# Two graph layers of an attention block, worked on two pairs of heads at a time, with all engine queues in a new order

## The chip, the cores and the metric

The kernel runs on one core of a Trainium2 chip. The metric is the device time of one execution in microseconds (us); less is better. TensorE (PE) multiplies, VectorE (DVE) and ScalarE (ACT) work on what it leaves in its accumulators (PSUM, eight banks of 128 partitions x 512 f32), GpSimd (POOL) does elementwise work in SBUF and issues indirect DMAs, SyncE (SP) issues the other DMAs. Every engine has one queue and works it off in order; semaphores tie the queues together.

## The reference

`x` is 16 batches of 256 tokens x 128. An attention block with a small graph network on its value vectors is added to it, then a mixture of experts (8 experts, the best 2 for each token). Cut to what matters here:

```python
xn = layer_norm(_layernorm(x), gamma_in)
q, k, v = (xn @ Wq) * scale, xn @ Wk, xn @ Wv          # 16 heads of 64
attn = softmax(causal(q @ k.T))
out = attn @ v
adj = clip(attn + eye(n), 0, 1)
deg = adj.sum(-1, keepdims=True)
feats = v
for l in range(2):                                     # the two graph layers
    h = feats @ gnn_w[l] + gnn_b[l]
    h = (adj @ h) / deg
    feats = gelu(h + feats)
out = out + feats @ lin_w + lin_b
x = x + layer_norm(out @ Wo, gamma_out)
x = x + moe(rmsnorm(_layernorm(x)))                    # router, top 2 of 8, silu(gate) * up, down
```

## The kernel before

One program without a scheduler: each engine has a function `batch(b, before, routed, after)` that lists, by hand, what this engine does for one batch, and the order of the lines is the order of its queue. Batches 0 and 1 and the last (15) are written out, batches 2 to 14 are one hardware loop. Beside the attention of batch `b` each turn carries the end of the batch before it (its last output products, the norm and residual steps `norm_tokens(before, 0..11)`), the routing of the one before that (`logits`, `choose`, `places`, `place_tokens`, `scatter`) and the input norm of the next one (`norm_step(after, 0..5)`, `x_transposed`, the first `queries_keys` and `values`). After batch 15 comes `sorted_stage`, the experts, in 71 steps of 128 tokens each.

The 16 heads of a batch are eight pairs n = 0 to 7. For a pair: `queries_keys(n)` (six f32r products of 256 columns into bank 0, copied by ACT), `scores(n)` (PE, 12 instructions, into two of the banks 1, 2, 6), `maxima(n, a)` (DVE), `exps(n, a)` (ACT, accumulating the sums), `adjacency(n)` and `weights(n)` (DVE), `graph(n)` and `degrees(n)` (POOL scales the exponentials and spreads the degrees), `transposes(n)` (PE, banks 3 and 4) and their copy `graph(n)` (ACT), `differences(n)` (PE, the graph applied to the values, bank 5) with `degrees(n)` (PE), `difference(n)` and `attended(n)` (DVE), and `mixed_values(n)` (ACT copies the mixed values from bank 5 to `gvT`).

Then the two layers. Before the change they too go pair by pair: `layer1(n)` (PE: `gvT` by the first weights, 256 columns in bank 0), `layer1_out(n)` (DVE adds the values to it, `z1`), `gelu1(n)` (ACT, `f1T`), `layer2_in(n)` (PE, two tiles of 128 columns in bank 2; ACT copies them to `g1`), `layer2(n)` (PE: the graph again, through `mixed`, 256 columns in bank 1), `layer2_out(n)` (DVE, `z2`), `gelu2(n)` (ACT, `f2T`), and `output_graph(n)` (PE, adds into bank 7 beside `output_attended(n)`). An f32 product of 256 columns is recorded as two MATMUL rows. `scores`, `differences` and `layer2` use 64 of the array's rows or columns per instruction, the rest uses 128.

What waits for what, as far as the prediction uses it: `scores(n)` needs `exps(n-1, 0)`, because three banks hold the scores; `differences(n)` needs the copies `graph(n)` and `mixed_values(n-1)`; `layer2(n)` needs ACT's copy of `layer2_in(n)` and `layer2_out(n-1)` of DVE; `output_natural` needs `output_bias` of DVE; POOL's queue waits for `place_tokens(routed, 1)` of DVE ahead of its four `scatter` DMAs. In batch 15 DVE also builds the table of expert steps (`table_first(0..4)`) and the high parts of the expert weights (`gate_up_high(0..7)`), POOL their low parts (`gate_up_low`), each of whose buffers SP refills by DMA when POOL has used it; SP loads the first tokens of the sorted stage (`zin`) when `table_first(4)` is done.

## Time and profile before

| | us |
|---|---|
| median of 3 runs | 1151.72 (1150.24 to 1152.72) |
| the profiled execution, its own time | 1155.31 |
| its span, first to last instruction | 1153.4 |
| PE, DVE, ACT, POOL busy of the span | 1071.1, 884.1, 803.4, 500.3 |
| mean granted clock of TensorE | 0.977 |

The span is what the trace shows; 1.9 us lie around it. Busy shares are averages over three stages: a start of some 20 us, sixteen batches of about 57 us (the last one longer), and the experts from about 958 us on. A row of the timeline has the start in the span, the duration, and in brackets the time that the engine sat idle before it and what ended that. Rows of PE overlap, since the ends are modelled; two starts subtracted tell more than a duration.

### The profile page before, as it was taken

Reading aid. Unit: us, or ns where it says so; the run is one execution under the profiler, and the core shown is the slowest. Engines: PE = TensorE matmul, PEld = TensorE weight load, DVE = VectorE, ACT = ScalarE, POOL = GpSimd, SP = SyncE. Lnnn points to the kernel's source line nnn. Section 1 sums busy time; section 2 is a strip of 40 time slices with the busy share of each in tenths; the row PEclk is TensorE's granted clock in tenths of the full one; section 3 lists DMA queues with packets and bytes.
Section 4 is the critical chain, followed back from the end, with each engine's and each line's share of the span. In section 5 each row is a group of like instructions: output and inputs, shape, how many; then the busy total and the mean of one; then the engine's idle time right before and its main releaser. Section 6 shows DMA issues by size and latency. Waiting matters only on the chain.

```text
span 1153.4 us, 28732 instructions
## 1 busy us (share of the span) xinstructions
PE 1071.1 (93%) x8576; PEld 854.7 (74%) x8576; DVE 884.1 (77%) x3760; ACT 803.4 (70%) x2351; POOL 500.3 (43%) x649
## 2 busy tenths in 40 slices
PE   4899999999999999999999999999999968898993
PEld 3777777777777777777777777777777747898993
DVE  3667797979797979797979797979797984565556
ACT  3668686868686868686868686868787735464551
POOL 3334244434343535353534353535353552544444
PEclk9899999999999999999999999999999988998997
DMA  6970000000000000000000000000000021222227
GB/s 192 405 260 2 1 2 11 1 10 1 10 1 11 1 10 0 10 0 10 0 10 0 10 0 10 0 10 0 10 0 10 2 78 44 56 57 61 59 61 226
DMA packets 37312, 47.43 MB, mean 41 GB/s; under 512 B 6009, under 2 KB 28539, under 8 KB 37200
## 3 DMA queue, kind: packets, MB, share of 16 engines
q1 hardware_dynamic: 32880, 37.81, 10.3%
q0 software_dynamic: 4320, 8.47, 2.2%
q14 instruction: 84, 0.69, 0.2%
q8 instruction: 28, 0.46, 0.2%
HBM read 18.14 MB, written 28.58 MB: 41 GB/s over the span
## 4 chain that ended last, share of the span: by engine, by line
PE 83%; DVE 6%; issue 3%; ACT 2%; SPq 2%; DMA 1%; another core or an unknown queue 1%; POOL 0%; DVEq 0%; POOLq 0%; ACTq 0%
PE bank L635 68%; PE bank L735 3%; PE bank L748 3%; PE bank L774 2%; PE bank L751 2%; PE bank L749 2%; PE bank L1006 2%; DMA x_all<-in_x 1%; PE bank L988 1%; DVE eb L1421 1%; DVE x_all L1995 1%; DVE got L1993 1%; DVE nmax L1406 0%; PE bank L783 0%
## 5 line engine op out<-in xcount | busy, mean ns | idle before, releaser
L497 POOL TENSOR_TENSOR ea<-ea,wgt 128x256 f32<-128x256 f32 x128 | 80.0, 625 | 429.6 <-DVE wgt L1430 396.1
L1406 DVE TENSOR_REDUCE nmax<-bank 128x1 f32<-128x128 f32 (+1 forms) x512 | 152.2, 347 | 66.0 <-PE bank L635 57.1
L499 POOL TENSOR_TENSOR eb<-eb,wgt 128x512 f32<-128x512 f32 x128 | 133.6, 1044 | 0.0
L635 PE MATMUL bank<-gt,g 128*64 128x256 f32 (+1 forms) x1024 | 112.0, 339 | 19.5 <-DVE z L1461 12.0
L1421 DVE SCALAR_TENSOR_TENSOR eb<-idw,ssum,eb 128x256 f32<-128x256 f32 x256 | 129.8, 544 | 0.0
L1124 ACT ACTIVATE ea<-bank,nmax 128x128 f32<-128x128 f32 x256 | 95.8, 374 | 47.9 <-DVE nmax L1406 45.9
L1124 ACT ACTIVATE eb<-bank,nmax 128x256 f32<-128x256 f32 x256 | 123.4, 482 | 0.0
L1092 ACT ACTIVATE gt<-bank 128x512 f32<-128x512 f32 (+1 forms) x256 | 111.7, 493 | 13.3 <-PE bank L751 11.8
L635 PE MATMUL bank<-gt,vnat 128*64 128x256 f32 (+1 forms) x1024 | 110.0, 335 | 3.0 <-issue 0.8
L635 PE MATMUL bank<-qk 64*128 64x128 f32 (+1 forms) x1024 | 112.7, 339 | 0.0
L525 POOL DMA_INDIRECT pairs<-zout,zin x71 | 69.7, 981 | 99.0 <-DVE zout L1954 89.3
L635 PEld LDWEIGHTS bank<-gt,g 128*64 128x64 f32 x1024 | 66.5, 137 | 61.4 <-issue 35.4
L1092 ACT ACTIVATE g<-bank 128x256 f32<-128x256 f32 x128 | 48.8, 381 | 84.8 <-PE bank L635 84.8
L635 PEld LDWEIGHTS bank<-gt,vnat 128*64 128x64 f32 x1024 | 65.1, 136 | 50.2 <-issue 17.0
L1461 DVE TENSOR_TENSOR z<-bank,f1T 128x256 f32<-128x256 f32 x128 | 53.6, 419 | 48.5 <-PE bank L635 48.5
L635 PE MATMUL bank<-xt_lo,w_hi 128*128 128x256 f32 x256 | 87.0, 340 | 1.9 <-DVE xt_lo L1399 1.9
L635 PE MATMUL bank<-gw,f1T 128*128 128x128 f32 x512 | 88.1, 295 | 0.3 <-ACT f1T L1148 0.3
L1947 DVE TENSOR_TENSOR shid<-bank,ssg 128x352 f32<-128x352 f32 x71 | 37.3, 525 | 63.5 <-ACT ssg L1272 40.6
L1092 ACT ACTIVATE qk<-bank 128x512 f32<-128x512 f32 x128 | 78.1, 610 | 11.2 <-PE bank L635 8.9
L635 PEld LDWEIGHTS bank<-gw,f1T 128*128 128x128 f32 x512 | 70.3, 192 | 19.3 <-issue 11.0
L1418 DVE SCALAR_TENSOR_TENSOR ea<-ident,ssum,ea 128x128 f32<-128x128 f32 x256 | 83.2, 362 | 0.0
L1092 ACT ACTIVATE gvT<-bank 128x256 f32<-128x256 f32 x128 | 49.1, 383 | 44.2 <-DVE aT L1440 40.6
(234 smaller groups left out, 3153.0 us busy)
## 6 DMA issues: line engine op xcount, KB each, us to landing
slots<-zero SPq DMA_DIRECT2D x33, 520.0 KB, 15.0
zin<-slots SPq DMA_DIRECT2D x71, 65.0 KB
got<-pairs SPq DMA_DIRECT2D x8, 512.0 KB, 5.5
raw_gu<-in_guT SPq DMA_DIRECT2D x8, 352.0 KB, 3.0
out<-x_all SPq DMA_DIRECT2D x8, 256.0 KB, 2.7
pairs<-zout,zin POOLq DMA_INDIRECT x71
dn<-in_downT SPq DMA_DIRECT2D x2, 512.0 KB, 16.0
slots<-z,row_now POOLq DMA_INDIRECT x64
```

The lines of the kernel that those rows point to most:

```text
L497: nc.gpsimd.tensor_tensor(ea[:, s], ea[:, s], wgt[:, s, 0:2].unsqueeze(2).to_broadcast([P, 2, P]), ALU.mult)
L499: nc.gpsimd.tensor_tensor(eb[:, s], eb[:, s], wgt[:, s, 2:4].unsqueeze(2).to_broadcast([P, 2, 2 * P]), ALU.mult).then_inc(p_g.sem, 1)
L525: nc.gpsimd.indirect_dma_start(pairs, bass.IndirectOffsetOnAxis(ap=zin[:, j % RING, ID:ID + 1].bitcast(u32), axis=0), zout[:, j % RING, :] ...
L635: return nc_mm(o, st, mo, start=first, stop=last, **more)
L735: mm = nc.tensor.transpose(o[:, m * TOKENS + t * P:m * TOKENS + (t + 1) * P], vnat[:, t, n * P:(n + 1) * P], ident[:, :])
L1092: return nc.scalar.activation(o, i, ACT.Copy, **more)
L1124: done = nc.scalar.activation(e[:, s, a, :], score_bank(n, a)[:, TILE_SCORES[t]], ACT.Exp, bias=nmax[:, s, i:i + 1], accum_out=ssum[:, s, ...
L1406: done = V.tensor_reduce(nmax[:, n % 3, i:i + 1], score_bank(n, a)[:, TILE_SCORES[t]], X, ALU.max, negate=True)
L1418: V.scalar_tensor_tensor(ea[:, s, a, :], ident[:, :], ssum[:, s, a:a + 1], ea[:, s, a, :], ALU.mult, ALU.max, accum_out=den[:, s, a:a + 1])
L1421: done = V.scalar_tensor_tensor(eb[:, s, a, :], idw[:, :], ssum[:, s, 2 + a:3 + a], eb[:, s, a, :], ALU.mult, ALU.max, accum_out=den[:, s, ...
L1461: V.tensor_tensor(z2[:, n % 2, :], bank[L2_BANK][:, 0:TOKENS], f1T[:, n % 4, :], ALU.add).then_inc(d_z2.sem, 1)
L1947: V.tensor_tensor(shid[:, j % 2, 0:HID], bank[2 + j % 2][:, 0:HID], ssg[:, j % 2, :], ALU.mult).then_inc(d_hid.sem, 1)
```

## The change

Both layers take a double d = 0 to 3, two pairs of heads, in place of a pair n:

- `layer1(d)`, `layer2_in(d)` and `layer2(d)` issue on PE the same products as before for two pairs one after the other, into one bank of 512 columns, with one signal at the end. `layer1_out`, `layer2_out` (DVE), `gelu1`, `gelu2` and the copy `layer2_in` (ACT) each become one instruction of 512 columns in place of two of 256: four of each in a batch, where there were eight.
- `gvT` is a ring of four pairs in place of eight slots, so `mixed_values(n)` for n >= 4 waits until `layer1` has read its slot. The banks of the last double are 4 and 3 in place of 2 and 1. `xn` goes (the second norm writes `xh` in place), `sq4` goes (its squares go into `y_now`), and `zero` lies in `gu_lo`.
- The queues of PE, ACT, DVE and POOL are written in a new order. The same work stands in them.

The diff, cut to its core:

```diff
-        L1_BANK, L2_IN_BANK, L2_BANK = 0, 2, 1
+        L1_BANK, L2_IN_BANKS, L2_BANKS = 0, (2, 2, 2, 4), (1, 1, 1, 3)
...
-            def layer2(b, n):
-                a_g1.wait(pe, b, n + 1)
-                if n >= 1:
-                    d_z2.wait(pe, b, n)
-                mixed(bank[L2_BANK][:, 0:TOKENS],
-                      lambda t, a: g1[:, n % 2, t, a * DHEAD:(a + 1) * DHEAD], n).then_inc(s_h2.sem, 1)
+            def layer2(b, d):
+                a_g1.wait(pe, b, d + 1)
+                if L2_BANKS[d] in (3, 4):
+                    a_gt.wait(pe, b, PAIRS)
+                if d >= 1:
+                    d_z2.wait(pe, b, d)
+                for m in range(2):
+                    mm = mixed(bank[L2_BANKS[d]][:, m * TOKENS:(m + 1) * TOKENS],
+                               lambda t, a: g1[:, d % 2, m, t, a * DHEAD:(a + 1) * DHEAD], 2 * d + m)
+                mm.then_inc(s_h2.sem, 1)
...
             def mixed_values(b, n):
                 d_a.wait(act, b, n + 1)
-                copy(gvT[:, n, :], bank[5][:, MIX]).then_inc(a_d.sem, 1)
+                if n >= 4:
+                    s_f1.wait(act, b, n // 2 - 1)
+                copy(gvT[:, n % 4, :], bank[5][:, MIX]).then_inc(a_d.sem, 1)
...
+            def layer1_out(b, d):
+                s_f1.wait(dve, b, d + 1)
+                if d >= 2:
+                    a_f1.wait(dve, b, d - 1)
+                V.tensor_tensor(z1[:, d % 2, :].rearrange("p (n i) -> p n i", n=2),
+                                bank[L1_BANK][:, :].rearrange("p (n i) -> p n i", n=2), vT[:, 2 * d:2 * d + 2, :],
+                                ALU.add).then_inc(d_z1.sem, 1)
```

Three places of the new order.

VectorE, the first third of a batch, from `adjacency(1)` to the reductions of pair 4. Before (the reductions into `nmax` are `maxima`, `rs` begins `adjacency`, `wgt` is `weights`, `topi` to `eq_bf` is `choose(routed, 1)`, `dT` and `aT` are `difference(0)` and `attended(0)`, `yT` is `output_bias`):

```order
L1430 RECIPROCAL wgt<-den 128x4
L1406 TENSOR_REDUCE nmax<-bank1 128x1 x2
L1747 MAX_INDEX topi<-top,lg 128x8 x2
L70 REGISTER_ALU
L1750 CAST topf<-topi 128x4
L70 REGISTER_ALU
L1755 TENSOR_TENSOR eq<-iot,topf 128x16 x2
```

```order
L1421 SCALAR_TENSOR_TENSOR eb,den<-idw,ssum,eb 128x256 x2
L1435 TENSOR_TENSOR dT<-bank5,vT 128x256
L1430 RECIPROCAL wgt<-den 128x4
L1406 TENSOR_REDUCE nmax<-bank2 128x1 x2
L1440 TENSOR_TENSOR aT<-bank5,dT 128x256
L1444 TENSOR_SCALAR yT<-bank7,yb 128x256
L70 REGISTER_ALU
L1406 TENSOR_REDUCE nmax<-bank6 128x1 x2
```

The same two stretches now:

```order
L1425 RECIPROCAL wgt<-den 128x4
L1731 MAX_INDEX topi<-top,lg 128x8 x2
L71 REGISTER_ALU
L1734 CAST topf<-topi 128x4
L71 REGISTER_ALU
L1739 TENSOR_TENSOR eq<-iot,topf 128x16 x2
```

```order
L1411 RECIPROCAL rs<-ssum 128x4
L1413 SCALAR_TENSOR_TENSOR ea,den<-ident,ssum,ea 128x128 x2
L1416 SCALAR_TENSOR_TENSOR eb,den<-idw,ssum,eb 128x256 x2
L71 REGISTER_ALU
L1411 RECIPROCAL rs<-ssum 128x4
L1413 SCALAR_TENSOR_TENSOR ea,den<-ident,ssum,ea 128x128 x2
L1416 SCALAR_TENSOR_TENSOR eb,den<-idw,ssum,eb 128x256 x2
L1425 RECIPROCAL wgt<-den 128x4
```

The routing's `choose(1)` stood behind `weights(0)` and a reduction; it now stands right behind `weights(1)`, which releases POOL's `graph(1)`. `adjacency(2)` and `adjacency(3)` now follow each other ahead of the reductions of pair 4, and `difference(0)`, `output_bias` and `attended(0)`, which stood ahead of them, come after the first of these.

TensorE, the place where the graph is applied in both layers, about two thirds into a batch. Before (`gt,vnat` is `differences`, `gt,g1` is `layer2`, `gw,f1T` is `layer2_in`):

```order
L635 MATMUL bank1<-gt0,g1 64x256 x2
L635 MATMUL bank1<-gt1,g1 64x128 x2
L635 MATMUL bank5<-gt0,vnat 64x256 x2
L635 MATMUL bank5<-gt1,vnat 64x128 x2
L635 MATMUL bank1<-gt0,g1 64x256 x2
L635 MATMUL bank1<-gt1,g1 64x128 x2
L635 MATMUL bank2<-gw,f1T 128x128 x2
```

and now:

```order
L634 MATMUL bank5<-gt0,vnat 64x256 x2
L634 MATMUL bank5<-gt1,vnat 64x128 x2
L634 MATMUL bank1<-gt0,g1 64x256 x2
L634 MATMUL bank1<-gt1,g1 64x128 x2
L634 MATMUL bank1<-gt0,g1 64x256 x2
L634 MATMUL bank1<-gt1,g1 64x128 x2
L777 MATMUL bank5<-ident,deg 128x128 x2
L634 MATMUL bank2<-gw,f1T 128x128 x4
```

Before, a product of the first layer's graph stands between two of the second's, and the second of these waits for DVE and ACT to have taken the first; now both pairs of a double stand together, with no wait between them.

VectorE in batch 15, around the building of the expert table. Before (`z2` is `layer2_out`, `passed_by` is the first row of `table_first(1)`, `gu_hi` is `gate_up_high`):

```order
L1837 TENSOR_TENSOR passed_by<-upto,tiles_full 128x64
L1841 TENSOR_REDUCE last_step<-passed_by 128x8
L1842 TENSOR_SCALAR gap_to<-tiles_full 128x8
L1461 TENSOR_TENSOR z2<-bank1,f1T 128x256
L1468 CAST gu_hi<-raw_gu 128x704
```

and now:

```order
L1465 CAST gu_hi<-raw_gu 128x704 x2
L1821 TENSOR_TENSOR passed_by<-upto,tiles_full 128x64
L1825 TENSOR_REDUCE last_step<-passed_by 128x8
L1826 TENSOR_SCALAR gap_to<-tiles_full 128x8
L1830 TENSOR_TENSOR passed<-last_step,step_no 128x384
L1833 TENSOR_REDUCE step_f<-passed 128x48
L1835 CAST step_expert<-step_f 128x48
L1430 TENSOR_TENSOR dT<-bank5,vT 128x256
```

The table's parts 1 and 2 now stand together behind two weight casts and ahead of `difference(7)`; part 0 stands in the same way behind casts 0 and 1 and ahead of `difference(6)`, part 4 behind the last cast.

## Rows read from the trace of the kernel before

**Rows 1.** The page: busy time of each engine and its share.
```profile
PE 1071.1 (93%) x8576; PEld 854.7 (74%) x8576; DVE 884.1 (77%) x3760; ACT 803.4 (70%) x2351; POOL 500.3 (43%) x649
```

**Rows 2.** Busy time by stretch: one batch (three stretches summed), then batch 15.
```profile
sum 57.00, PE 56.14 PEld 43.22 DVE 47.67 ACT 43.63 POOL 24.96; mean PE 18.71 PEld 14.41 DVE 15.89 ACT 14.54 POOL 8.32
...
883.70:957.60 73.90, 62.46 (x465) 47.26 (x463) 61.24 (x224) 43.35 (x132) 37.23 (x39) 0.91 0.15 41
```

**Rows 3.** One line's instructions, 190 to 880 us: duration min/median/max, first and last start.
```profile
L1399 DVE SCALAR_TENSOR_TENSOR xt_lo<-bank,gin,xt_hi x13: 483/484/485, 192.3 to 877.7; 128x256 fp32r<-128x256 f32 x13
```

**Rows 4.** Groups by form, 195 to 910 us: busy, mean ns | idle before.
```profile
L635 PE MATMUL bank<-gt,g 128*64 128x256 f32 x388 | 62.7, 400 | 9.1 <-issue 6.4 <-DVE z L1461 2.6
...
L1461 DVE TENSOR_TENSOR z<-bank,f1T 128x256 f32<-128x256 f32 x98 | 41.1, 419 | 39.0 <-PE bank L635 39.0
```

**Rows 5.** Timeline of PE in one batch: start, duration, engine and operation.
```profile
409.69 0.87 PE L635 MATMUL bank<-gt,g 128*64 128x256 f32 x8
410.39 0.82 PE L635 MATMUL bank<-gt,vnat 128*64 128x256 f32 x8
411.85 0.87 PE L635 MATMUL bank<-gt,g 128*64 128x256 f32 x8 [0.64 <-issue]
...
440.36 0.87 PE L635 MATMUL bank<-gt,vnat 128*64 128x256 f32 x8
441.16 0.33 PE L748 MATMUL bank<-ident,ea 128*128 128x128 f32 x1
```

**Rows 6.** Groups by form, all of the span: the widest f32 addition of DVE.
```profile
L1947 DVE TENSOR_TENSOR shid<-bank,ssg 128x352 f32<-128x352 f32 x71 | 37.3, 525 | 63.5 <-ACT ssg L1272 40.6 <-PE bank L635 19.4 <-remote 2.2
```

**Rows 7.** Timeline of DVE, the start of the next batch.
```profile
429.35 1.15 DVE L1406 TENSOR_REDUCE nmax<-bank 128x1 f32<-128x128 f32 x4 [2.80 <-PE bank L635]
...
432.20 0.18 DVE L1416 RECIPROCAL rs<-ssum 128x4 f32<-128x4 f32 x1
...
433.63 0.62 DVE L1406 TENSOR_REDUCE nmax<-bank 128x1 f32<-128x128 f32 x2
...
434.76 0.08 DVE L1747 MATCH_VALUE_LOAD topi<-top,lg 128x8 f32 x1
...
435.15 0.89 DVE L1750 CAST topf<-topi 128x4 f32<-128x4 uint32 x1
...
436.84 0.62 DVE L1406 TENSOR_REDUCE nmax<-bank 128x1 f32<-128x128 f32 x2
```

**Rows 8.** Timeline of DVE, then of PE, up to the scores of pair 5.
```profile
443.24 0.42 DVE L1435 TENSOR_TENSOR dT<-bank,vT 128x256 f32<-128x256 f32 x1
...
444.17 0.41 DVE L1440 TENSOR_TENSOR aT<-bank,dT 128x256 f32<-128x256 f32 x1
444.50 0.47 DVE L1444 TENSOR_SCALAR yT<-bank,yb 128x256 f32<-128x256 f32 x1
445.22 0.62 DVE L1406 TENSOR_REDUCE nmax<-bank 128x1 f32<-128x128 f32 x2 [0.25 <-PE bank L635]
...
447.89 0.28 PE L635 MATMUL bank<-mask,pick 64*128 64x128 bf16 x4
```

**Rows 9.** All instructions of two DVE lines: duration ns min/median/max, first and last start.
```profile
L1750 DVE CAST topf<-topi x16: 170/892/895, 148.5 to 1025.1; 128x4 f32<-128x4 uint32 x16
...
L1421 DVE SCALAR_TENSOR_TENSOR eb<-idw,ssum,eb x256: 473/480/1249, 29.8 to 921.3; 128x256 f32<-128x256 f32 x128
```

**Rows 10.** Timeline of POOL beside the rows of DVE in rows 7.
```profile
434.98 1.04 POOL L499 TENSOR_TENSOR eb<-eb,wgt 128x512 f32<-128x512 f32 x1
```

**Rows 11.** Timelines of batch 15: DVE, PE, SP's DMA queue.
```profile
926.12 4.47 DVE L1837 TENSOR_TENSOR passed_by<-upto,tiles_full 128x64 f32<-128x64 f32 x1
...
931.39 1.55 PE L635 MATMUL bank<-gt,g 128*64 128x256 f32 x8 [5.10 <-DVE z L1461]
...
952.28 4.06 SPq L403 DMA_DIRECT2D zin<-slots  x8
...
957.59 0.27 PE L988 MATMUL bank<-ident,zin 128*128 128x128 f32 x1
```

507 lines of the change are left out of this document (239 added, 268 removed).

## The prediction

> **What bounds the kernel now.** The page comes first: PE is busy 1071.1 us of the span, DVE 884.1, ACT 803.4 [rows 1]. The stages say more. The reader should see in the table by stretch that in one batch of 57.00 us PE is busy 56.14 and DVE 47.67, and that in batch 15 PE is busy only 62.46 of 73.90 us at a granted clock of 0.91 [rows 2]. So a batch is bound by the number and the kind of PE instructions, and a faster DVE or ACT is worth only what PE waits. The length of a turn follows from one DVE instruction that stands once in each batch: (877.7 - 192.3) / 12 = 57.12 us [rows 3]. Thirteen turns of the loop make two thirds of the time.
>
> How much does PE wait in a turn? The table shows 57.00 - 56.14 = 0.86 us idle [rows 2], nearly all of it ahead of `layer2` (9.1 us in 715) [rows 4]. But rows of PE overlap: from 410.39 to 411.85 there are 1.46 us between two starts, where the same step takes 0.70 without a wait (409.69 to 410.39), so 0.76 is lost and 0.64 shown [rows 5]. 0.86 x 0.76 / 0.64 = 1.0 us, and waits of under 0.3 us show not at all; I take 1.3 us a turn, between 0.9 and 2.0.
>
> **The change part by part.**
>
> Merged instructions. An addition of 256 columns takes 419 ns [rows 4], one of 352 takes 525 [rows 6]; that is 1.1 ns a column, so one of 512 comes to about 700 ns (estimate), 2 x 419 - 700 = 0.14 us less. Eight pairs of them become eight single ones in a batch: 1.1 us less on DVE, and ACT saves on twelve. Neither is the bound, so none of this is in the sum by itself. It costs latency: the chain from `layer1` to `layer2_in` moves in steps of two pairs. PE has other work beside it, so I put nothing there; if that cover were gone it would be 0.3 us a double, 1.1 us a batch, at most.
>
> PE's own work. The products are the same. What changes is how often PE goes between instructions on 64 and on 128 rows: `differences` ahead of `layer2` takes 0.70 us, ahead of `transposes` 0.80 (440.36 to 441.16) [rows 5], so a change costs about 0.10 on leaving, and about as much again on entering and on the first product behind. With both pairs of a double together I count 15 stretches of the 64 kind in a turn in place of 16: -0.25 us (0.1 to 0.3).
>
> Old waits. The wait ahead of the second `layer2` goes, since the pairs of a double stand together and DVE's `layer2_out` has two doubles' time: -1.3 us. What is late next is the question, and the new order answers it with DVE.
>
> New wait at the scores of pair 5. DVE's queue from its first reduction (429.35) to the reductions of pair 4 (445.22) is 15.9 us long [rows 7, 8]. In the new order `adjacency(3)` comes in ahead of them, 1.43 us (432.20 to 433.63) [rows 7], and `difference(0)`, `attended(0)` and `output_bias` leave, 0.42 + 0.41 + 0.47 less 0.08 each for their overlap = 1.06 [rows 8]: +0.4. `choose(1)` takes 2.08 now (434.76 to 436.84) of which its cast of 4 elements is 0.89 [rows 7]; the same cast takes 0.17 when nothing is in its way [rows 9], and here it ends with POOL's instruction (434.98 + 1.04 = 436.02) [rows 10]. In the new order it stands right behind `weights(1)`, which starts POOL's `graph(1)` and two `degrees` in one row. `choose(2)` now stands free of POOL. Bounds for both together: -1.4 us if neither is held up, +1.2 if the four small instructions are held one by one; I take +0.2, since today's place is of the same kind. Since `choose(1)` no longer fills the wait for `scores(2)`, about 0.7 of idle time comes in (0.3 to 0.9, by hand along PE's queue). DVE's idle time of 2.80 us at the turn of the loop [rows 7] begins earlier against PE, as DVE's last addition stands 0.6 us further ahead: -0.4. And 0.25 of idle time ahead of 445.22 [rows 8] is used up. Together +0.65 us: those reductions start about 16.5 us behind DVE's first, their reductions and exponentials add 1.5. PE meanwhile has one `transposes`, one `differences` (0.80) and one `degrees` less and one output product more ahead of `scores(5)`, 1.2 us less work. It stands ready some 1.2 us ahead of today's 447.89 [rows 8], and DVE with ACT lets it go about 0.6 ahead of that (429.35 + 16.5 + 1.5 = 447.35): a wait of 0.6 us (0 to 1.1) that is not there today.
>
> New wait at `differences(2)`. `norm_tokens(1)` and the late `attended(0)` and `attended(1)` stand in DVE's queue between `output_bias` and `mixed_values(1)`, which releases it. Along the queue I find 5.5 to 5.9 us from the start of `scores(5)` where PE needs 5.3: 0.4 us (0 to 0.8). Behind it `differences(4)` waits for exponentials 7 and `mixed_values(3)`: 0.15 us (0 to 0.4). The four scatters now go ahead of `degrees(5)` and `graph(6)` on POOL; `transposes(6)` then finds its operand ready with little to spare, and I count nothing.
>
> A turn: 57.12 - 1.3 - 0.25 + 0.6 + 0.4 + 0.15 = 56.7 us, -0.4 in each. Thirteen turns: -5.2 us. Batches 0 and 1 have no `choose` in their front: -0.75 each.
>
> Batch 15. It has 73.90 - 62.46 = 11.4 us of idle PE [rows 2], the greatest part behind one DVE instruction of the table that took 4.47 us beside four POOL instructions in a row, and made PE wait 5.10 [rows 11]. The new order bunches: `table_first(0)` with two casts ahead of `difference(6)`, parts 1 and 2 with two casts ahead of `difference(7)`, part 3 ahead of the last norm step, each with POOL's `gate_up_low` running. By hand: PE waits about 4 us ahead of `differences(7)`, 5 ahead of `layer1(3)`, 4 ahead of `tokens_transposed`, in place of today's 11.4. The table's last part, after which SP issues the loads (952.28) that PE takes up at 957.59 [rows 11], comes behind the last cast, so the experts begin later. +3 us (-3 to +8).
>
> The sum, on the profiled execution's own 1155.3: -5.2 - 1.5 + 3 = -3.7, 1151.6. That execution stands 3.6 us above the median of the runs, so a median of **1148.0 us**, 0.3% less. A difference of 0.2% is about what a measurement of this kernel can tell from none: 1149.4 to 1154.0.
>
> **The rivals.**
>
> A, the waits do go. If the reductions of pair 4 are not late (choose unhindered, idle time at the turn shorter), only 0.3 us of new waits remain: a turn of 55.9, -1.25 x 13 = -16, and with -1.5 and +2: 1136. For it: DVE has 9 us of idle time in a turn [rows 2] and 1.1 us less to do. Against it: that idle time lies in the last third, and the front is where `adjacency(3)` was put.
>
> B, the waits only move. The new waits equal the old (1.55 in place of 1.15): a turn of 57.1, nothing gained in the loop, 1153 with batch 15. For it: DVE's front holds +0.65 by my own count.
>
> C, the slower side: DVE's small instructions are held by POOL. The cast went from 0.17 to 0.89 and the worst `adjacency` instruction from 0.48 to 1.249 [rows 9] beside a POOL instruction, and the one of 4.47 us let four go by [rows 11]. If `choose(1)` is held through `graph(1)` and both `degrees`, it lasts 3.3 us in place of 2.1, `scores(3)` to (5) slip with it, `norm_tokens(1)` behind `weights(4)` meets `graph(4)` in the same way and `adjacency(5)` the two `degrees` behind it: +0.8 to +1 us a turn against the forecast, a turn of 57.5, and 1148.0 + 0.85 x 13 = 1159. It decides from a `choose(1)` of about 3 us and cannot be told from today's trace, where such meetings are mostly single.
>
> The Trainium skill (GPSIMD Engine Reference, section Specifications) says that POOL shares its SBUF interfaces with VectorE and that DVE instructions with two SBUF inputs, or in a two-port mode, contend with it. By that rule the casts, the comparisons and the `adjacency` instructions are touched and reductions from PSUM are not; the trace agrees (0.17 against 0.89). It gives the additions of rival C, and speaks against this order.
>
> D, batch 15 alone goes wrong or right by its bounds: +5 or -6 on the forecast, 1153 or 1142. It shifts the others and is in the range.
>
> **How the numbers follow.** Forecast, 1143 to 1152: chance 0.45, of which 0.37 below 1149.4 and 0.08 within 0.2%. A, 1132 to 1142: 0.17. B, 1150 to 1156: 0.20, of which 0.12 within 0.2% and 0.08 above. C, 1155 to 1166: 0.18, all above. Faster 0.37 + 0.17 = 0.54, same 0.08 + 0.12 = 0.20, slower 0.08 + 0.18 = 0.26. The range of 8 in 10 is 1134 to 1161: it leaves out the outer half of A and of C.
>
> **What would show it.** Right: turns of 56.7 us by the same DVE line; a PE wait of about half a us ahead of the scores of pair 5, put down to ACT's exponentials; no wait of 0.6 ahead of `layer2`; `choose(1)` of 2 to 2.7 us; the cast near 0.3 to 0.9; PE idle for about 13 us in batch 15. C shows as a `choose(1)` of 3 us and `adjacency` instructions of 0.8 and 1.2 us more often than today; A as scores of pair 5 that wait for nothing. What would make it wrong: an instruction of 512 columns far from 700 ns; a wait on the chain from `layer1` to `layer2_in`, which I counted at nothing; POOL late for `transposes(5)` or (6) behind the scatters; and a granted clock that falls in a longer wait of batch 15.

## The result, and the profile after

The changed kernel took 1156.84 us in the median of four runs (1155.25 to 1158.43), the kernel before 1150.98 in the same comparison (1148.45 to 1152.72): a ratio of 1.0045, 95% interval 1.0027 to 1.0064, slower where the forecast was faster. The time lies inside the forecast's range (1134 to 1161), the direction is wrong. Five repeats in other sets of runs, each on one chip, gave 0.9972, 1.0033, 0.9976, 1.0123 and 0.9976: of the six, three are a little faster and three slower. That is the first thing to explain. Two things come out below: a loss in batch 15, whose cause is shown, and signals of TensorE that come late in three of the six sets, whose cause stays open.

The page: TensorE has 8 us less of busy time than in [rows 1], ScalarE 28, VectorE 10.

```profile
PE 1063.3 (92%) x8576; PEld 858.9 (74%) x8576; DVE 874.4 (76%) x3632; ACT 775.3 (67%) x2159; POOL 508.3 (44%) x649
```

The DVE instruction that stands once in a batch, as in [rows 3] (duration min/median/max, first and last start of 13):

```profile
L1394 DVE SCALAR_TENSOR_TENSOR xt_lo<-bank,gin,xt_hi x13: 473/475/476, 189.4 to 870.8; 128x256 fp32r<-128x256 f32 x13
```

The turn is (870.8 - 189.4) / 12 = 56.78 us, 0.34 shorter than 57.12, and batch 15 begins 6.9 us earlier than before. Now busy time by stretch, of the changed kernel for one turn and for batch 15 (from that DVE instruction to the first transpose of the experts' stage), then of the kernel before for the same batch 15. Columns: stretch, its length, busy PE, PEld, DVE, ACT, POOL, granted clock, share and rate of the DMAs.

```profile
359.64:416.37 56.73, 55.39 (x466) 43.27 (x464) 46.88 (x211) 42.10 (x121) 25.51 (x33) 1.00 0.01 5
870.83:957.88 87.05, 68.92 (x520) 52.40 (x516) 65.67 (x225) 44.63 (x125) 39.27 (x40) 0.91 0.11 31
```

```profile
877.72:957.59 79.87, 68.43 (x510) 51.80 (x507) 64.07 (x234) 47.36 (x141) 37.92 (x40) 0.91 0.14 38
```

Batch 15 is 87.05 us in place of 79.87: +7.2, nearly all of it idle TensorE (18.1 against 11.4 us; the rest is 0.5 us more of busy time). The turns' gain is spent there, and the first transpose of the experts' stage stands at 957.88 in place of 957.59 [rows 11]. The experts' stage is the same length in these two profiles (170.2 us from its first transpose to its last), so the two profiled executions took the same time, 1155.25 and 1155.31 us.

What TensorE waits for in batch 15 of the changed kernel, from its timeline:

```profile
927.02 1.55 PE L634 MATMUL bank<-gt,vnat 128*64 128x256 f32 x8 [4.27 <-ACT gvT L1096]
...
935.13 2.07 PE L634 MATMUL bank<-gvT,gw 128*128 128x256 f32 x4 [2.48 <-ACT gvT L1096]
...
945.82 0.69 PE L956 MATMUL bank<-ident,z 128*128 128x128 f32 x2 [5.00 <-DVE z L1707]
...
957.88 0.48 PE L991 MATMUL bank<-ident,zin 128*128 128x128 f32 x1 [4.74 <-DMA zin<-slots]
```

These are `differences(7)`, `layer1(3)`, `tokens_transposed` and the first expert step. On VectorE, small instructions of the table stand before each of them; on POOL's queue `gate_up_low` runs beside them:

```profile
921.57 1.64 DVE L1805 TENSOR_TENSOR used<-next_row,first_row 128x8 f32<-128x8 f32 x1
923.24 1.85 DVE L1797 TENSOR_TENSOR taken<-used,tile_to 128x256 f32<-128x256 f32 x1
...
929.20 1.69 DVE L1821 TENSOR_TENSOR passed_by<-upto,tiles_full 128x64 f32<-128x64 f32 x1
...
941.26 2.03 DVE L1839 TENSOR_TENSOR passed<-passed,gap_to 128x384 f32<-128x384 f32 x1
...
950.59 1.90 DVE L1797 TENSOR_TENSOR taken<-used,tile_from 128x256 f32<-128x256 f32 x1
```

```profile
921.29 3.51 POOL L538 TENSOR_TENSOR gu_lo<-raw_gu,gu_hi 128x704 fp32r<-128x704 f32 x2 [1.85 <-DVE gu_hi L1465]
...
940.99 3.83 POOL L538 TENSOR_TENSOR gu_lo<-raw_gu,gu_hi 128x704 fp32r<-128x704 f32 x2 [2.20 <-DVE gu_hi L1465]
950.32 3.70 POOL L538 TENSOR_TENSOR gu_lo<-raw_gu,gu_hi 128x704 fp32r<-128x704 f32 x2 [5.50 <-DVE gu_hi L1465]
```

An addition of 8 columns takes 1.64 us. In the loop, the places that the prediction spoke of, from the timelines of TensorE and VectorE:

```profile
442.28 0.44 PE L786 MATMUL bank<-ident,yT 128*128 128x128 f32 x2
442.65 0.28 PE L634 MATMUL bank<-mask,pick 64*128 64x128 bf16 x4
...
447.74 0.38 PE L754 MATMUL bank<-ident,eb 128*128 128x128 f32 x2
448.49 0.87 PE L634 MATMUL bank<-gt,vnat 128*64 128x256 f32 x8 [0.36 <-ACT gvT L1096]
...
460.08 1.52 PE L634 MATMUL bank<-gt,g 128*64 128x256 f32 x16 [0.70 <-issue]
```

```profile
433.84 0.06 DVE L1731 MATCH_VALUE_LOAD topi<-top,lg 128x8 f32 x1
...
434.21 0.42 DVE L1734 CAST topf<-topi 128x4 f32<-128x4 uint32 x1
434.67 1.06 DVE L1739 TENSOR_TENSOR eq<-iot,topf 128x16 f32<-128x16 f32 x2
...
436.16 1.14 DVE L1401 TENSOR_REDUCE nmax<-bank 128x1 f32<-128x128 f32 x4
```

The scores of pair 5 (442.65) follow their forerunner without a wait that the timeline shows; by the starts, 0.13 us are lost. `differences(2)` (448.49) waits: 1.24 us from the start of the transposes ahead of it, where 0.75 is the least seen in the loop, so 0.5 a turn. The wait of 0.70 ahead of `layer2(0)` at 460.08 was not in the prediction. `choose(1)` takes 433.84 to 436.16, 2.3 us. Section 4 of the page, the chain of work that ended last, has VectorE at 24% of the span, where it had 6% before. The page before, then the page after:

```profile
PE 83%; DVE 6%; issue 3%; ACT 2%; SPq 2%; DMA 1%; another core or an unknown queue 1%; POOL 0%; DVEq 0%; POOLq 0%; ACTq 0%
```

```profile
PE 65%; DVE 24%; issue 6%; ACT 2%; SPq 2%; DMA 1%; DVEq 0%; another core or an unknown queue 0%
```

In the turn shown above the chain runs along VectorE's queue from 431.1 us to the `attended(1)` that ends at 447.9, and from there over ScalarE's copy to `differences(2)`.

### The profile page after: what moved, and what is told of

The parts are those of the page before. It is cut to its first block, busy times and chain, and to the rows that moved or that the text cites. A ratio compares the mean times of both kernels' runs of the same rounds, so it can differ in the third digit from the quotient of the medians.

```text
span 1153.5 us, 28149 instructions
## 1 busy us (share of the span) xinstructions
PE 1063.3 (92%) x8576; PEld 858.9 (74%) x8576; DVE 874.4 (76%) x3632; ACT 775.3 (67%) x2159; POOL 508.3 (44%) x649
## 4 chain that ended last, share of the span: by engine, by line
PE 65%; DVE 24%; issue 6%; ACT 2%; SPq 2%; DMA 1%; DVEq 0%; another core or an unknown queue 0%
PE bank L634 54%; DVE nmax L1401 6%; DVE eb L1416 5%; DVE ea L1413 3%; PE bank L777 3%; PE bank L1009 2%; PE bank L738 1%; DVE aT L1435 1%; PE bank L751 1%; PE bank L754 1%; PE bank L752 1%; DVE dT L1430 1%; DMA x_all<-in_x 1%; PE bank L991 1%; ACT gvT L1096 1%
## 5 line engine op out<-in xcount | busy, mean ns | idle before, releaser
L1401 DVE TENSOR_REDUCE nmax<-bank 128x1 f32<-128x128 f32 (+1 forms) x512 | 148.9, 344 | 68.0 <-PE bank L634 68.0
L634 PE MATMUL bank<-gt,vnat 128*64 128x256 f32 (+1 forms) x1024 | 112.1, 338 | 14.3 <-ACT gvT L1096 11.2
L1416 DVE SCALAR_TENSOR_TENSOR eb<-idw,ssum,eb 128x256 f32<-128x256 f32 x256 | 124.2, 521 | 0.0
L634 PEld LDWEIGHTS bank<-gt,vnat 128*64 128x64 f32 x1024 | 67.9, 136 | 61.3 <-issue 39.8
L634 PE MATMUL bank<-qk 64*128 64x128 f32 (+1 forms) x1024 | 112.9, 340 | 0.0
L634 PE MATMUL bank<-gt,g 128*64 128x256 f32 (+1 forms) x1024 | 98.6, 335 | 9.7 <-issue 8.3
L634 PEld LDWEIGHTS bank<-gt,g 128*64 128x64 f32 x1024 | 64.8, 138 | 42.7 <-issue 20.9
L1096 ACT ACTIVATE qk<-bank 128x512 f32<-128x512 f32 x128 | 76.7, 599 | 21.5 <-PE bank L634 21.5
L634 PE MATMUL bank<-xt_lo,w_hi 128*128 128x256 f32 x256 | 88.5, 346 | 2.4 <-DVE xt_lo L1394 2.1
L1931 DVE TENSOR_TENSOR shid<-bank,ssg 128x352 f32<-128x352 f32 x71 | 37.2, 524 | 66.0 <-ACT ssg L1267 45.0
L514 POOL TENSOR_TENSOR rs<-ve,half 128x2 f32<-128x2 f32 x48 | 34.7, 722 | 113.7 <-DVE ve L1697 62.3
L507 POOL TENSOR_TENSOR deg<-den,rs 128x256 f32<-128x256 f32 x128 | 82.3, 652 | 0.3
L1458 DVE TENSOR_TENSOR z<-bank,f1T 128x512 f32<-128x512 f32 x64 | 44.0, 688 | 48.4 <-PE bank L634 48.3
L1413 DVE SCALAR_TENSOR_TENSOR ea<-ident,ssum,ea 128x128 f32<-128x128 f32 x256 | 78.1, 341 | 0.0
L634 PE MATMUL bank<-aT,wo_sb 128*128 128x256 f32 x256 | 78.0, 388 | 0.0
## 6 DMA issues: line engine op xcount, KB each, us to landing
dn<-in_downT SPq DMA_DIRECT2D x2, 512.0 KB, 15.8
```

The lines of the kernel that those rows point to most:

```text
L507: nc.gpsimd.tensor_tensor(deg[:, s], den[:, s, :].unsqueeze(2).to_broadcast([P, 4, DHEAD]), rs[:, s, :].unsqueeze(2).to_broadcast([P, 4, D ...
L634: return nc_mm(o, st, mo, start=first, stop=last, **more)
L1096: return nc.scalar.activation(o, i, ACT.Copy, **more)
L1401: done = V.tensor_reduce(nmax[:, n % 3, i:i + 1], score_bank(n, a)[:, TILE_SCORES[t]], X, ALU.max, negate=True)
L1413: V.scalar_tensor_tensor(ea[:, s, a, :], ident[:, :], ssum[:, s, a:a + 1], ea[:, s, a, :], ALU.mult, ALU.max, accum_out=den[:, s, a:a + 1])
L1416: done = V.scalar_tensor_tensor(eb[:, s, a, :], idw[:, :], ssum[:, s, 2 + a:3 + a], eb[:, s, a, :], ALU.mult, ALU.max, accum_out=den[:, s, ...
```

## The experiments

First the two kernels again, unchanged, with more runs and a second profile of each.

> The kernel before, unchanged, for a second profile of it. Its first profiled execution took 1155.3 us, its timed runs 1150.98. Theory 1: that execution was a long one of its kind, in the experts' stage, where the granted clock dipped; a second profile then shows turns of 57.1 us again, the first expert step at 957 to 958, and a span some 3 to 4 us shorter, from a higher clock behind 958. Theory 2: a profiled execution of this kernel is always that much longer; then it stands again 3 to 4 us above the timed runs.

> The changed kernel, unchanged, for a second profile of it and more runs. Both theories: turns of 56.75 us, batch 15 (from its second-norm row on DVE to the first expert step) 87.0 us as against 79.9 before, ratio of the runs to before 1.0045. Theory 1 (chance in the experts' stage): its profile lies within 2 us of its timed runs, on either side. Theory 2: 3 to 4 us above them.

Measured on one chip: before 1147.1 us (23 runs, 1142.9 to 1151.6), changed 1144.7 (12 runs, 1140.9 to 1145.7), ratio 0.9972 (0.9958 to 0.9987): faster. b_again's profiled execution took 1146.8, at the median of its kernel's runs, so theory 2 is out. a_again's took 1141.1, 3.6 us under its median, where theory 1 had at most 2: one profiled execution stands anywhere within some 4 us of its median. Batch 15 is 78.1 us before and 85.4 after, +7.2 once more. But the turn of the changed kernel is 56.26, not 56.78, while that of the kernel before hardly moves (57.02 against 57.12).

```profile
L1394 DVE SCALAR_TENSOR_TENSOR xt_lo<-bank,gin,xt_hi x13: 473/476/476, 190.7 to 865.8; 128x256 fp32r<-128x256 f32 x13
```

Half a microsecond of each turn differs between two profiles of one program. Here is ScalarE's timeline in the same turn, of the first profile of the changed kernel and then of a_again; up to these rows the two run alike to 0.02 us, counted from the first reduction of the turn:

```profile
457.98 0.38 ACT L1096 ACTIVATE gvT<-bank 128x256 f32<-128x256 f32 x1
459.43 0.60 ACT L1096 ACTIVATE g<-bank 128x512 f32<-128x512 f32 x1 [1.07 <-PE bank L634]
```

```profile
457.38 0.38 ACT L1096 ACTIVATE gvT<-bank 128x256 f32<-128x256 f32 x1
457.77 0.60 ACT L1096 ACTIVATE g<-bank 128x512 f32<-128x512 f32 x1
```

ScalarE's copy behind `layer2_in(0)` begins 1.05 us late. TensorE's products for it start at the same place in both, and TensorE goes on to its next product at the same time. It is late in batches 3 to 15, by 1.0 us, once by 1.7; `layer2(0)` waits for it, hence the 0.70 at 460.08. I call it the late copy. ScalarE itself is not what is late: the row names `PE bank L634` as what ended its wait, and the trace has the time of TensorE's signal, the semaphore event at the end of `layer2_in(0)`. In a_again it stands 0.29 us behind the start of the last product in every batch; in the first profile it stands 0.29 us behind it in batches 0 and 1 and 1.2 to 1.4 us behind it, once 1.97, in the eleven later batches that have it recorded. In batches 3 to 15 ScalarE begins 0.02 us behind the signal in both. So the late copy is a late signal of TensorE. More on it behind batch 15.

### Batch 15

a_t4 moves one part of the table, a_spread takes the bunching apart:

```diff
 layer2_out(b, 3)
-gate_up_high(6), gate_up_high(7)
 table_first(4)
+gate_up_high(6), gate_up_high(7)
```

```diff
 layer1_out(b, 1)
+table_first(0)
 difference(b, 5)
...
 gate_up_high(0), gate_up_high(1)
-table_first(0)
 difference(b, 6)
...
-gate_up_high(2), gate_up_high(3), table_first(1), table_first(2)
 difference(b, 7)
 attended(b, 7)
+table_first(1), table_first(2), gate_up_high(2), gate_up_high(3)
...
 layer2_out(b, 2)
-gate_up_high(4), gate_up_high(5), table_first(3)
 norm_tokens(before, 11)
+table_first(3), table_first(4), gate_up_high(4), gate_up_high(5)
 layer2_out(b, 3)
 gate_up_high(6), gate_up_high(7)
-table_first(4)
```

> The changed kernel with the last part of the expert table (table_first(4)) ahead of the last two weight casts of VectorE, in place of behind them. Theory A: the wait of 4.7 us ahead of the first expert step is that table part, which stands behind two casts of 0.47 and beside two GpSimd instructions of 1.85; without them it ends at about 951 in place of 954, SP issues the loads 2.5 to 3.3 us earlier, and the kernel is 2.5 to 3.3 us faster than the changed one: about 1154. Rival B: the start of the experts hangs on GpSimd's last gate_up_low as well, which then ends 1.5 us later than now; nothing or less than 1 us is gained: 1156 to 1157.

> The changed kernel with batch 15's table and weight casts no longer bunched ahead of difference(6) and difference(7): table_first(0) in VectorE's idle time ahead of difference(5), parts 1 and 2 and casts 2 and 3 behind attended(7), parts 3 and 4 behind the last norm step and ahead of casts 4 and 5. The turns are untouched. Theory A (the bunching is what batch 15 lost): the waits ahead of differences(7) (4.3), layer1(3) (2.5), tokens_transposed (5.0) and the first expert step (4.7) shrink to 5 to 9 us together, 8 to 11 us less: 1145 to 1149, faster than the kernel before. Rival B: the same work on VectorE and GpSimd only moves the waits, or GpSimd's gate_up_low chain becomes the end: less than 4 us gained, 1153 or more.

a_t4: 1139.3 us, ratio 0.9924 (0.9902 to 0.9947), 5.5 under a_again beside it. The wait ahead of the first expert step falls from 3.5 to 1.4 us and batch 15 from 85.4 to 83.7; 1.7 us, between what B had (under 1) and what A had (2.5 to 3.3). The median gained more than A had. So the table's last part holds up the start of the experts, and its size is not settled by this run.

a_spread: 1134.1 us, 0.9889 (0.9865 to 0.9912), 10.6 under a_again: A, at its upper end. Batch 15 is 76.7 us. What is left of its waits is one of 4.8 us, ahead of `layer2_in(3)`. The chain goes back to a norm instruction of VectorE that takes 3.32 us for two halves of 0.3, beside two `gate_up_low` of GpSimd. TensorE, then VectorE:

```profile
929.31 2.08 PE L634 MATMUL bank<-gw,f1T 128*128 128x128 f32 x8 [4.78 <-ACT f1T L1154]
```

```profile
923.69 3.32 DVE L1648 TENSOR_SCALAR t<-x_all,mv,rs 128x128 f32<-128x128 f32 x2
```

Is it the place in the queue or GpSimd that costs? a_nolow leaves the place and takes the work of GpSimd away; b_bunch gives the kernel before the new placing and nothing else.

```diff
-nc.gpsimd.tensor_tensor(gu_lo[:, e, :], raw_gu[:, e % 2, :], gu_hi[:, e, :].bitcast(f32),
+nc.gpsimd.tensor_tensor(gu_lo[:, e, 0:8], raw_gu[:, e % 2, 0:8], gu_hi[:, e, 0:8].bitcast(f32),
```

> The changed kernel with GpSimd's eight gate_up_low subtractions cut from 704 columns to 8 (a memset of the low parts ahead of batch 15 stands in for them, so the low halves of the expert weights are left out). Order and signals stay. In the profile of the changed kernel eight small VectorE instructions of the table and one norm addition take 1.0 to 2.0 us beside them, where the same forms take 0.15 to 0.55 elsewhere: about 10 us in all. Theory A (GpSimd holds VectorE up, and that is what the bunching costs): these rows fall to 0.15 to 0.6, the waits ahead of differences(7), layer1(3) and tokens_transposed fall from 12 us to under 5, batch 15 gets 7 to 10 us shorter. Rival B (the place in VectorE's queue is the cost, held or not): batch 15 gets shorter by under 3 us, the waits stay at 9 or more.

> The kernel before, with nothing of the change but the placing of batch 15: table_first(0) with casts 0 and 1 ahead of difference(6), parts 1 and 2 with casts 2 and 3 ahead of difference(7), part 3 with casts 4 and 5 ahead of the last norm step, part 4 behind the last cast, and GpSimd's gate_up_low in the changed kernel's groups. Theory A (the placing lost the 7.2 us of batch 15, whatever the width of the layers' instructions): batch 15 goes from 78 to 80 us to 85 to 88, 5 to 8 us slower than before: ratio 1.005 to 1.007. Rival B (the doubles in the drain of the last batch are the cost, since each chain step now moves two pairs): less than 2 us slower.

a_nolow (1151.2 us, ratio 0.9992, 0.9978 to 1.0006): the same VectorE instructions in the same places, from its timeline:

```profile
928.25 0.17 DVE L1806 TENSOR_TENSOR used<-next_row,first_row 128x8 f32<-128x8 f32 x1
928.45 0.45 DVE L1798 TENSOR_TENSOR taken<-used,tile_to 128x256 f32<-128x256 f32 x1
...
933.01 0.22 DVE L1822 TENSOR_TENSOR passed_by<-upto,tiles_full 128x64 f32<-128x64 f32 x1
...
940.76 0.56 DVE L1840 TENSOR_TENSOR passed<-passed,gap_to 128x384 f32<-128x384 f32 x1
```

1.64, 1.85, 1.69 and 2.03 us became 0.17, 0.45, 0.22 and 0.56. Batch 15 is 79.4 us where a_third beside it has 87.0, though the memset put in ahead of it costs a wait of 3.6 us that the others don't have. With that wait added back it would be about 11 us (an estimate, 7.6 + 3.6). Not all of it need be the holding of VectorE, since GpSimd's shorter instructions also free the weight buffers sooner. The waits ahead of `differences(7)`, `layer1(3)` and `tokens_transposed` are 1.4, 2.0 and 2.8 us, 6.1 in place of 11.8. Theory A, with a little more left than it said.

b_bunch: 1161.0 us, ratio 1.0074 (1.0055 to 1.0092); its batch 15 is 86.6 us, where the kernel before has 78.1 and 79.9. With layers still pair by pair, the placing alone brings the whole loss: A, and B (the doubles) is out. TensorE's waits in it:

```profile
935.13 1.22 PE L635 MATMUL bank<-gvT,gw 128*128 128x256 f32 x2 [5.41 <-ACT gvT L1092]
946.87 1.22 PE L635 MATMUL bank<-gvT,gw 128*128 128x256 f32 x2 [4.45 <-ACT gvT L1092]
953.90 0.69 PE L953 MATMUL bank<-ident,z 128*128 128x128 f32 x2 [3.17 <-DVE z L1714]
964.32 0.33 PE L988 MATMUL bank<-ident,zin 128*128 128x128 f32 x1 [2.98 <-DMA zin<-slots]
```

Not every VectorE instruction is held. In a_again's trace reciprocals of 128x4 take 0.16 to 0.17 us beside a wide GpSimd instruction and 0.16 to 0.18 alone, and batch-norm statistics of 128x128 take 0.27 to 0.29 both ways, though both read SBUF. Nor does every GpSimd instruction hold: beside its power steps of two columns 14 VectorE additions of 128x256 take 0.42 to 0.43 us, and beside its scatters 42 `adjacency` instructions of 128x128 take 0.31 to 0.35, as they do alone.

That GpSimd holds VectorE agrees with what the Trainium skill (GPSIMD Engine Reference, section Specifications) says of shared SBUF interfaces: held are additions of two SBUF tiles and the f32 norm step of one; `layer2_out`, which reads PSUM, takes 0.68 to 0.69 us beside GpSimd and alone. The Trainium skill (VectorE: DVE Perf Modes, section "The TRN2 errata") gives 691 ns for an f32 addition of 512 columns; the trace has 688 in the mean of 64, and the prediction's 700 was near enough.

### The loop, and the late copy

```diff
 weights(b, 4)
-norm_tokens(before, 1)
 attended(b, 1)
+norm_tokens(before, 1)
 maxima(b, 6, 0)
```

> The changed kernel, unchanged, a third time, since its turn of the loop was 56.78 us in its first profile and 56.26 in its second. The difference is one stretch: ScalarE's copy after layer2_in(0) began 1.0 us later in 12 of the 13 turns of the first, with the copies ahead of it and TensorE's products at the same places to 0.02 us. Theory S (a stall of ScalarE that comes with the execution, not with the order): the turn is again either 56.3 or 56.8 us, nothing between, and the late copy goes with the 56.8. Theory T (a race in the order that slips by small amounts): turns between the two, or other rows late. By either, the time from the last turn to the first expert step is 85 to 87 us. Ratio to before 0.997 without the stall, 1.003 with it.

> The kernel a_spread with one more edit, in the turns: norm_tokens(1) of VectorE behind attended(1) in place of ahead of it. Theory A: the wait of 0.5 us in each turn ahead of differences(2) (1.24 us from transposes to differences where 0.75 is the least) is the 0.7 us of norm_tokens(1) with its addition held up by GpSimd's graph(3); without it the wait goes and a turn is 0.4 to 0.5 us shorter: 55.8, and 6 us less than a_spread in all, 1128 on the chip where that took 1134. Rival B: what is late next (ScalarE's gvT copy behind an exponential, or the scores of pair 6, since maxima(6) comes no earlier) takes it: under 0.15 us a turn, under 2 us in all.

a_third: 1157.4 us, ratio 1.0033 (1.0016 to 1.0049), a turn of 56.86 us and the copy late in batches 3 to 15, by 1.0 us or 1.7, nothing between: theory S. a_norm1, in the same set: 1142.2 us, 0.9904 (0.9887 to 0.9921), a turn of 56.43, 0.43 less than a_third's: A. The wait ahead of `differences(2)` fell from 0.50 to 0.25 us a turn.

Next, whether the late copy hangs on a place in ScalarE's program. a_pad24 (and later a_pad8) put 24 (8) one-column copies ahead of batch 1 on ScalarE; a_scat moves the scatters of GpSimd:

```diff
+for i in range(24):
+    copy(warm[:, i:i + 1], half[:, 0:1])
 batch(1, 0, None, 2)
```

```diff
 graph(b, 5)
-scatter(routed, 0..3)
 degrees(b, 5)
 graph(b, 6)
+scatter(routed, 0..3)
```

> The changed kernel, unchanged, as the control of the two kernels beside it. On a chip that shows ScalarE's stall (two of three so far) its turn is 56.8 us with the copy behind layer2_in(0) 1.0 us late in 12 of 13 turns; without the stall 56.3 us and nothing late.

> The changed kernel with 24 one-column copies of ScalarE put in ahead of batch 1 (some 5 to 6 us of ScalarE once, outside the loop). ScalarE's work in the loop, and all other queues, are as in the changed kernel, but each of its instructions stands 24 places further in its program. Only to be read where the control shows the stall. Theory P (the stall hangs on a place in ScalarE's program, as code that comes late would): it goes to an instruction about 24 places earlier in the turn, an exponential or a copy of the attention part, or vanishes; the copy behind layer2_in(0) is on time. Theory E (it hangs on what happens at that moment, such as the scatters of GpSimd that end when the copy begins, or TensorE's signal that comes as ScalarE gets there): it stays at the copy behind layer2_in(0), 1.0 us late, turn 56.8.

> The changed kernel with GpSimd's four scatters behind graph(6) in every batch, in place of behind graph(5), some 2.9 us later in the turn. ScalarE's program is untouched. Only to be read where the control shows the stall. Theory E with the scatters as the event: the copy behind layer2_in(0) is on time, and another instruction is late beside the last scatter, or none. Theory P: the same copy is 1.0 us late as in the control. Without the stall: a turn of 56.3 to 56.6 us either way.

This chip didn't show it: a_fourth 0.9976 (0.9959 to 0.9992), a turn of 56.26, nothing late. a_pad24 (1.0003, turn 56.27) says nothing. a_scat was meant for the late copy alone, and I had its turn at 56.3 to 56.6; it is 58.7, the ratio 1.0286 (1.0253 to 1.0318). By its list of waits TensorE now waits 22.4 us for ScalarE's copies of mixed values and 5.6 for `graph` of POOL in 11 turns. Moving the four scatters by one pair's work costs 2.4 us a turn in this order: they hold POOL for 5 us, and `degrees(6)` and `graph(7)` stand behind them.

> The changed kernel, unchanged, as the control once more: two of four profiles so far show ScalarE's copy behind layer2_in(0) 1.0 us late in each turn but the first (turn 56.8 us), two do not (56.26). If it is late here, the two kernels beside it can be read; if it is not, they say nothing of the stall, as the two with that aim in the call before.

> The changed kernel with the 24 one-column copies of ScalarE ahead of batch 1, again, for a chip where the control shows the stall. Theory P (a place in ScalarE's program): the late instruction is about 24 places earlier in the turn or there is none; the copy behind layer2_in(0) is on time, a turn of 56.3 to 56.6 us. Theory E (what happens at that moment): the same copy is late, turn 56.8.

> The same with 8 copies in place of 24. Theory P: the late instruction stands 8 places earlier than in the control, which in ScalarE's program are the two exponentials of pair 7 and the copies behind them. Theory E: the same copy as in the control is late.

Another chip, and here the copy is late, by 1.15 or 1.9 us; c_control has a turn of 57.61 us and a ratio of 1.0123 (1.0083 to 1.0163). In c_pad24 (turn 57.50) and c_pad8 (57.47) the same copy is late by the same two amounts. So it isn't the place in the program: theory P is out. What goes with it: in all seven profiles of the changed kernel and its variants that show it, it is late in batches 3 to 15 (in batch 2 in some), which have scatters, batch 15 standing outside the loop, and never in batches 0 and 1, which have none. The scatters' last one runs from 42.1 to 43.1 us of the turn, the copy is due at 42.0 and begins at 43.0 to 43.2 or 43.7 to 43.9. In the experts' stage the same four scatters stand at two places, and there too ScalarE's instructions come late in the first profile of the changed kernel:

```profile
987.10 0.37 ACT L1096 ACTIVATE sz_hi<-bank,normw 128x128 fp32r<-128x128 f32 x1 [1.03 <-remote]
990.73 0.49 ACT L1096 ACTIVATE shT<-bank 128x384 f32<-128x384 f32 x1 [3.27 <-remote]
```

Again it is TensorE's signals: the one that the first row waits for stands at 987.07, 1.55 us behind the end of its transpose, and that of the second at 990.71, 4.2 us behind the end of its products, and ScalarE begins 0.02 to 0.03 us behind each. The two expert steps behind the scatters take 7.3 and 8.4 us in place of 2.07; in a_again 3.5 and 4.7. That is why the experts' stage is 169 to 172 us in the profiles of the changed kernel and its variants with the late copy, and 161.5 to 167.4 in those without.

Is it only the changed kernel? All 20 profiles can be asked for signals that stand over 0.3 us behind the end of the instruction that gives them. In 11 profiles there is none. In the other 9 there are 24 to 45, all of them TensorE's, most beside scatters. These 9 are all profiles of three sets of runs, the first, the one of a_third and the one of c_control. The old order is among them: in the kernel before's first profile 22 signals of `layer2` come 0.6 to 1.4 us late in batches 2 to 14, in b_bunch 25 of them, in b_again none. The same 9 profiles lack about 1,300 of 4,600 events of landed DMAs, which the others have, and where the event that ended a wait is among the missing ones the row says `<-remote`. So it goes with the set of runs and meets either kernel. It isn't a trait of one chip as far as the record tells: the sets of a_third (late) and d_control (on time) carry the same chip number.

The two kernels pay differently, since their late signals stand at different places. TensorE's wait ahead of `layer2` in the kernel before goes from 0.64 us a turn (b_again) to 0.77 (first profile), a turn from 57.02 to 57.12; in the changed kernel a turn goes from 56.26 to 56.78. In the experts' stage both pay, 6.0 and 7.6 us. From the on-time to the late profile the span grows from 1144.9 to 1153.4 us before the change and from 1139.3 to 1153.5 after it.

> The changed kernel, unchanged, as the control. In every profile that shows the stall, ScalarE's copy behind layer2_in(0) is late in batches 2 to 15, all those with scatters, also in batch 15, which stands outside the loop; in batches 0 and 1, without scatters, it never is. 24 or 8 more instructions ahead of it did not move it. So it goes with what happens at that moment. Late by 1.0 to 1.9 us if this chip shows it.

> The changed kernel with the four scatters behind graph(6), where the turn was 58.7 us on a chip without the stall and the copy behind layer2_in(0) on time. Only to be read for the stall where the control shows it. If the scatters are what ScalarE is held by: an instruction of ScalarE beside or just behind the last of the scatters, now at 43 to 49 us of the turn, is late, and the copy behind layer2_in(0), which now comes before them, is on time. If not: the copy is late as in the control.

> The fastest kernel so far (0.984 of the kernel before on a chip without the stall), again. On a chip with the stall its turn is 0.5 us longer, 56.4 in place of 55.9, and the ratio 0.989 to 0.990 where the control has 1.003 to 1.004; without it 0.984 again.

No late copy this time (0.9976, turn 56.27; d_scat 1.0264, turn 58.7), so that the one test of the scatters as its cause could not be read. The late signals go with the scatters; that these cause them, and by what, stays open.

### The fastest version

a_dvelow is a_norm1 with `gate_up_low` on VectorE, behind its casts:

```diff
-pool: gate_up_low(0..7)
 gate_up_high(0), gate_up_high(1)
+dve:  gate_up_low(0), gate_up_low(1)
 ... and so for 2 to 7
```

> The kernel a_norm1 with gate_up_low moved from GpSimd to VectorE, right behind the casts it belongs to: nothing of GpSimd's but its two power steps then runs beside the end of batch 15. Theory A (each gate_up_low on GpSimd holds a VectorE instruction for up to its 1.75 us, and the wait of 4.8 us ahead of layer2_in(3) in a_spread is a norm instruction of 0.6 us that took 3.3): VectorE pays 8 times about 0.8 us and gets back about 8, and the chain of loads gets shorter; batch 15 from 76.2 to 73 to 75 us, 1 to 3 us faster than a_norm1. Rival B (VectorE is the tighter queue, 6.4 us more of its own work counts in full where the holds were partly idle time): batch 15 of 78 to 80, 2 to 4 us slower than a_norm1.

1127.6 us, ratio 0.9842 (0.9817 to 0.9866), and 1125.6, 0.9828 (0.9799 to 0.9858), on the second chip: 1.6 to 1.7% faster than the kernel before. Batch 15 is 74.3 us, as A had it (73 to 75), where a_norm1 has 76.2:

```profile
860.02:934.29 74.27, 65.64 (x521) 50.62 (x517) 62.46 (x231) 44.52 (x125) 24.57 (x32) 0.98 0.12 36
```

GpSimd is busy 12.6 us less than in a_spread's batch 15 (37.2), VectorE 0.75 more (61.7): eight subtractions moved to it cost it almost nothing net. How much the move gains is less sure. a_norm1 was measured only in a set with late signals, a_dvelow only in two without, and one kernel's batch 15 differs by up to 1.7 us between sets (85.4 to 87.1). Against the changed kernel of its own set, a_norm1 is 15.2 us faster, a_dvelow 15.8 and 18.0; so the move gains some 0.6 to 2.8 us (an estimate across sets). What is left with late signals was not measured.

## Why the prediction was wrong, step by step

The figures of all comparisons of the changed kernel, in us but for the ratio; "experts" is the stage's first transpose to its last:

| profile | ratio | turn | batch 15 | experts | copy late by |
|---|---|---|---|---|---|
| the first | 1.0045 | 56.78 | 87.1 | 170.2 | 1.0 |
| a_again | 0.9972 | 56.26 | 85.4 | 162.6 | 0 |
| a_third | 1.0033 | 56.86 | 87.0 | 170.8 | 1.0 |
| a_fourth | 0.9976 | 56.26 | 86.7 | 164.0 | 0 |
| c_control | 1.0123 | 57.61 | 87.1 | 171.8 | 1.2 or 1.9 |
| d_control | 0.9976 | 56.27 | 86.6 | 162.7 | 0 |
| before, first | | 57.12 | 79.9 | 170.2 | |
| b_again | | 57.02 | 78.1 | 164.2 | |

**Batch 15, the step of the sum that failed.** The prediction had +3 us (-3 to +8); it is +7.2, in both pairs of profiles. The three waits that it worked out were 4, 5 and 4 us, the trace has 4.3, 2.5 and 5.0: 11.8 against 13. What was mis-sized is the term behind them, that the experts begin later, of which 1.4 us was in the sum (3 less 13 - 11.4): TensorE waits 4.7 us for the first loads, since `table_first(4)` behind casts 6 and 7 is held as well. Another 1.6 us of idle time in small pieces were at nothing, since the sum set three waits against all of the idle time of before, and 0.5 us are busy time. -1.2 + 3.3 + 1.6 + 0.5 makes the 4.2 us by which the term was short. That the mechanism was seen and rival C priced it only for the loop is the lesson: the same holding in the table was there in [rows 11], with 4.47 us for one instruction (GpSimd had five instructions in a row beside it, not four).

**The turn, right in its sum and wrong in its parts.** Forecast 56.7; measured 56.78 with the late copy and 56.26 without. The old wait is gone: in a_again TensorE's list of waits for 11 turns holds one line, in us, times and longest:

```profile
PE bank L634 <- ACT gvT L1096: 6.4, 23, 0.4
```

Those 23 stand ahead of `differences(2)`, which loses 0.5 a turn (said 0.4), and of one more of its kind. The fewer changes between the two kinds of instruction (-0.25) were not measured apart, nor was what the doubles do in a turn apart from what the new order does: no run has one without the other. The scores of pair 5 wait 0.13, where 0.6 was said: DVE's queue was sized well (its reductions of pair 4 begin 16.8 us behind the first, said 16.5, and `choose(1)` is 2.3, as said), but TensorE gets there only at 18.6 us behind that same first reduction (442.65 against 424.07), where the prediction had 17.3. `differences(4)` waits for nothing (said 0.15). 57.12 - 1.3 - 0.25 + 0.13 + 0.5 = 56.2, what the profiles without the late copy show. With it, the signal that is 1.0 us late makes 0.5 a turn, of which the prediction had nothing, and by luck it fills the place of the waits that don't come. Batches 0 and 1 gained 2.5 us in the first pair of profiles and 1.2 in the second (said 1.5).

**The direction.** Without the late signals the ratio is 0.9972 to 0.9976, and the forecast was 0.997: right in size by luck, since two errors cancel, batch 15 some 4 us worse and the turns 13 x 0.44 = 6 us better. With them the changed kernel loses more than the old one. Its medians are 1156.8, 1157.4 and 1169.1 us in the three sets with late signals and 1144.7, 1143.4 and 1143.6 in the three without; those of the kernel before are 1151.0, 1152.3 and 1153.7 and 1147.1, 1147.1 and 1146.4. The recorded comparison is one with late signals. The prediction had no term for them, and the trace of before, which has them, showed them in the loop only as a part of its wait ahead of `layer2`. That they turn the sign is read from six comparisons that fall into two groups; what brings them is not known. Batch 15 is enough to turn it back: a_norm1, which has batch 15 taken apart and one edit in the loop, is at 0.9904 in a set with late signals.

**From the sum to 1148.0.** The forecast for the profiled execution was 1151.6 us, and it took 1155.25, 3.7 more: the 4.2 of batch 15, less small errors of the other terms. The forecast of the median then took 3.6 us off, as the distance of the profiled execution of before from its kernel's median. The profiled execution of the changed kernel stands 1.6 us under its median, so this step is off by 5.2 us, more than batch 15. In b_again the distance is 0.2 us, in a_again -3.6: it is chance, and was no term to carry over.

**The rivals.** A gave a turn of 55.9 if the reductions of pair 4 are not late. They are late as forecast; the scores of pair 5 hardly wait all the same, since TensorE comes later than forecast, but `differences(2)` does, and a_dvelow, with that wait halved, has 55.90. B named the size of the turn (57.1) more nearly than the forecast only for c_control (57.61), and not its cause. C was wrong in its place: `choose(1)` is 2.3 us, not 3, and no norm step of the loop costs TensorE more than the 0.5; but its mechanism, GpSimd holding VectorE, is what batch 15 lost by. D, batch 15 alone 5 us worse, is the nearest: 4.2 worse.

## What to carry to other kernels

Where the trace shows that two engines hold each other up, their work belongs apart in time, above all where one of them has a chain of tiny dependent instructions: count each as long as the other engine's instruction beside it, not as long as itself. A stage that stands once and takes 7% of the time can undo what is won in the loop; its placing wants the same care as the loop's. And where two kernels differ by half a percent, profile both more than once, in more than one set of runs, before a cause is looked for in the order. Where an instruction begins late though its forerunners ran on time, look for the time of the signal that it waits for, and not only for the end of the work.
